# Output projection of an attention layer: weights streamed in by output block instead of loaded whole before it

## The chip, the cores and the metric

The kernel runs on the 8 cores of one Trainium2 chip. All cores run the same program, each on its own batch element, with no exchange between them. The metric is the device time in microseconds of the slowest core.

## The reference, cut to what matters

```python
x = x + 0.5 * ffn(layernorm(x))      # low-rank FFN, gelu
x = x + attn(layernorm(x))           # causal, 16 heads of 64
x = x + 0.5 * ffn(layernorm(x))

# the last step of attn, the one that the change touches:
attn = jnp.einsum('bhqk,bkhd->bqhd', scores, v)
return jnp.einsum('bqhd,hdm->bqm', attn, O_w) + O_b
```

The input is 8 x 2048 x 1024 in float32: one sequence of 2048 positions and 1024 features for each core. `O_w` is 1024 x 1024 when its heads are flattened, `O_b` has 1024 elements.

## The kernel before, in words

The residual stream `x` stays in SBUF for the whole program as [128 partitions, 8 feature chunks, 2048 positions] in float32. The program is a sequence of stages: FFN sublayer `f1`, the attention sublayer, FFN sublayer `f2`, and the output DMAs. Each stage is made of `nc.Block()` regions. In a block each engine (TensorE, VectorE, ScalarE, GpSimd and SyncE, which issues all DMAs) has its own instruction list, written out by hand; within a block the lists are tied together only by semaphores, and at the end of a block all engines meet in a barrier before any of them goes on.

The attention sublayer (`emit_attn_sublayer`, from L1076 on) ends in eight head pairs (`emit_attn_pair`, one block each, L604). The last thing that the last pair does is to normalise its last 512 positions and to write them into `attn_fm` (L768), a bf16 tensor [128, 8 chunks of head features, 2048 positions] that holds the attention result.

Then comes the output projection, in three blocks:

- `load_stage` (from L335 on) with four pieces of `ow`, 1 MB each (two chunks of 128 rows, all 1024 output columns, so that every descriptor's row of `ow` is read in full). The staging tile `wst3` has room for exactly one piece, so SyncE's load of a piece (L360) waits for the cast of the piece before it (the wait at L359). VectorE casts each piece to bf16 into `wb2` (L373), which holds the whole weight.
- `load_stage` once more for the bias `ob`, 4 KB, cast into `r_ob`.
- The projection block (from L1361 on). Its order is eight output blocks `m` of 128 features, and in each the four position tiles of 512. One tile is eight matmuls over the chunks of `attn_fm` (L1374) and one of the bias (L1376) into one half of a double buffer in PSUM. VectorE then adds the tile to `x` (L1387), which frees the half (semaphore `EV`); TensorE signals each finished tile through `PE`. Output block `m` needs the columns 128m to 128m+127 of `ow` alone.

In the trace's rows the buffer numbers are left out, so `wb2` reads as `wb` and `wst3` as `wst`. After the projection block comes the statistics block of `f2` (loads at L208, first casts at L251).

One further load of the same form as the changed ones is in the kernel before: in each head pair SyncE loads 128 columns of `kw` into `wst4` as [128, 8, 128] (L857) once the cast of the `qw` piece (L799) has freed the buffer, and VectorE casts it (L802) when it has landed.

Of the kernel before, what the change touches and what calls it, by code (L numbers as in the profile page):

```python
# [8 lines left out]
BF16 = mybir.dt.bfloat16  # L9
# [5 lines left out]
D = 1024  # L15
NT = S // 128
NC = D // 128
# [13 lines left out]
def build_nc(debug=()):  # L31
    nc = bass.Bass("TRN2", target_bir_lowering=False, dynamic_dma_scratch_size=2048)

    din = {}
# [22 lines left out]
    def mk(stack, name, shape, dt=F32, psum=False):  # L57
        uid[0] += 1
        f = nc.psum_tensor if psum else nc.sbuf_tensor
        if _dbg_alloc and not psum:  # L60
            nb = int(np.prod(shape[1:])) * (4 if dt == F32 else 2)
            _tot[0] += nb

            @contextlib.contextmanager
            def _wrap(nb=nb, nm=name):
                with f(f"{nm}_{uid[0]}", shape, dt) as t:
                    print(f"+ {nm:12s} {nb:7d} tot={_tot[0]}")
                    try:
                        yield t
                    finally:  # L70
                        _tot[0] -= nb
                        print(f"- {nm:12s} tot={_tot[0]}")
            return stack.enter_context(_wrap())
        return stack.enter_context(f(f"{name}_{uid[0]}", shape, dt))

    with gctx:
# [20 lines left out]
        class _H:  # L97
# [9 lines left out]
        LD, CAST, PE, EV, ACT, ROW, ST, DMX, WC, WP = (_H(sems[k]) for k in  # L107
            ["ld", "cast", "pe", "ev", "act", "row", "st", "dmx", "wc", "wp"])
        LSL = [_H(sems[f"l{i}"]) for i in range(10)]
# [225 lines left out]
        def load_stage(stage, pairs, scale=None):  # L335
            views = []
            half = stage.shape[-1] // 2
            for i, (src_ap, dst_ap) in enumerate(pairs):
                fs = list(src_ap.shape[1:])
                tot = int(np.prod(fs))  # L340
                npart = src_ap.shape[0]
                if tot <= half and len(pairs) > 1:
                    sv = stage[0:npart, half * (i % 2):half * (i % 2) + tot]
                else:
                    sv = stage[0:npart, 0:tot]
                if len(fs) == 2:
                    sv = sv.rearrange("p (a b) -> p a b", a=fs[0])
                views.append(sv)
            dbl = all(int(np.prod(p[0].shape[1:])) <= half for p in pairs) and len(pairs) > 1
            with nc.Block() as blk:  # L350
                ld0, cast0 = LD.v, CAST.v
                n = len(pairs)

                @blk.sync
                def _(sync):
                    if not dbl:
                        for i in range(n):
                            if i >= 1:
                                sync.wait_ge(CAST.h, cast0 + i)  # L359
                            LD.inc(sync.dma_start(views[i], pairs[i][0]), 16)  # L360
                    else:
                        for g in range((n + 1) // 2):
                            if g >= 1:
                                sync.wait_ge(CAST.h, cast0 + 2 * g)
                            for i in (2 * g, 2 * g + 1):
                                if i < n:
                                    LD.inc(sync.dma_start(views[i], pairs[i][0]), 16)

                @blk.vector
                def _(vector):  # L370
                    def cast_one(i):
                        if scale is None:
                            CAST.inc(vector.tensor_copy(pairs[i][1], views[i]))  # L373
                        else:
                            CAST.inc(vector.tensor_scalar(pairs[i][1], views[i], scale, None, OP.mult))
                    if not dbl:
                        for i in range(n):
                            vector.wait_ge(LD.h, ld0 + 16 * (i + 1))
                            cast_one(i)
                    else:  # L380
                        for g in range((n + 1) // 2):
                            hi = min(n, 2 * g + 2)
                            vector.wait_ge(LD.h, ld0 + 16 * hi)
                            for i in range(2 * g, hi):
                                cast_one(i)
# [690 lines left out]
        def emit_attn_sublayer():  # L1076
            with contextlib.ExitStack() as actx:
# [30 lines left out]
                with nc.Block() as blk:  # L1108
                    @blk.sync
                    def _(sync):  # L1110
                        LD.inc(sync.dma_start(ct["m2t"][:, :], din["masksb"].ap()[1]), 16)
                        sync.wait_ge(LD.h, LD.v)
# [55 lines left out]
                with contextlib.ExitStack() as vctx:  # L1168
# [21 lines left out]
                    with nc.Block() as blk:  # L1190
                        pe0, ev0, row_lc, ld_vb = PE.v, EV.v, ROW.v, LD.v
# [42 lines left out]
                        def _(vector):  # L1234
# [53 lines left out]
                            for _, fn in sorted(dvepl, key=lambda x: x[0]):  # L1288
                                fn(vector)
# [60 lines left out]

                bctx.close()
                with contextlib.ExitStack() as octx:
                    wb2 = mk(octx, "wb2", [128, NC, D], BF16)
                    r_ob = mk(octx, "r_ob", [1, D], BF16)
                    wst3 = mk(octx, "wst3", [128, 2048])
                    load_stage(wst3, [(din["ow"].ap().rearrange("(c p) m -> p c m", p=128)
                                       [:, 2 * i:2 * (i + 1), :], wb2[:, 2 * i:2 * (i + 1), :])
                                      for i in range(4)])
                    load_stage(wst3, [(din["ob"].ap(), r_ob[0:1, :])])

                    with nc.Block() as blk:  # L1361
                        pe0, ev0 = PE.v, EV.v

                        @blk.tensor
                        def _(tensor):
                            i = 0
                            for m in range(NC):
                                for tci in range(NTC):
                                    if i >= 2:
                                        tensor.wait_ge(EV.h, ev0 + i - 1)  # L1370
                                    sl = slice(TC * tci, TC * (tci + 1))
                                    psl = p_big[:, 512 * (i % 2):512 * (i % 2) + TC]
                                    for hc in range(NC):
                                        tensor.matmul(psl, wb2[:, hc, 128 * m:128 * (m + 1)],  # L1374
                                                      ct["attn_fm"][:, hc, sl], start=(hc == 0), stop=False)
                                    PE.inc(tensor.matmul(psl, r_ob[0:1, 128 * m:128 * (m + 1)],  # L1376
                                                         r_ones[0:1, 0:TC], start=False, stop=True))
                                    i += 1

                        @blk.vector  # L1380
                        def _(vector, pe0=pe0):
                            i = 0
                            for m in range(NC):
                                for tci in range(NTC):
                                    vector.wait_ge(PE.h, pe0 + i + 1)
                                    sl = slice(TC * tci, TC * (tci + 1))
                                    EV.inc(vector.tensor_tensor(x[:, m, sl], x[:, m, sl],  # L1387
                                                                p_big[:, 512 * (i % 2):512 * (i % 2) + TC],
                                                                OP.add))
                                    i += 1  # L1390
# [12 lines left out]
        if PHASES >= 2:  # L1403
            emit_attn_sublayer()
            if "x2" in dbg:
                emit_dump_fm(dbg["x2"], x)
# [47 lines left out]
```

## Time and profile before

| | us |
|---|---|
| median of 2 runs | 2037.53 |
| lowest, highest | 2034.7, 2040.36 |
| profiled execution, its own time | 2036.73 |
| span of its slowest core (core 5) | 2035.2 |
| span of its fastest core (core 0) | 1995.6 |

| busy on core 5 | us | share of the span |
|---|---|---|
| TensorE matmuls (PE) | 1568.7 | 77% |
| VectorE (DVE) | 571.2 | 28% |
| ScalarE (ACT) | 557.2 | 27% |
| GpSimd (POOL) | 95.3 | 5% |

A span runs from a core's first instruction to its last. The profiled execution's own time is 1.5 us above the span of its slowest core. PE is TensorE's matmuls and PEld its weight loads. PEclk is the granted clock of TensorE: 1.00 is 2.4 GHz and 0.50 is 1.2 GHz, and a mean in between is a mixture of the two.

### The profile page before, as it was taken

What the parts mean: (1) busy time and instruction counts of PE and PEld (TensorE: products, weight loads), DVE (VectorE), ACT (ScalarE), POOL (GpSimd) and SP (SyncE); (2) the same over time, 40 slices, a digit from 0 to 9 for tenths busy, and PEclk for the clock granted to TensorE, in tenths of its full rate; (3) what the DMA queues carried; (4) which work ended last, traced back from release to release, by engine and by line L of the source; (5) the groups of instructions that cost most, each with busy time, mean ns of one, the idle gap of its engine ahead of it and who ended that gap; (6) DMA issues with size and microseconds to landing.
All of it is one profiled execution on the core that took longest, in us unless ns stands there. A gap on an engine that the chain in (4) does not pass through costs nothing. (4 is left out here: it accounts for less than half of the span.)

```text
span 2035.2 us, 17874 instructions; the slowest of 8 cores (1995.6 to 2035.2 us)
## 1 busy us (share of the span) xinstructions
PE 1568.7 (77%) x5640; PEld 418.2 (21%) x5640; DVE 571.2 (28%) x952; ACT 557.2 (27%) x615; POOL 95.3 (5%) x108
## 2 busy tenths in 40 slices
PE   2389997567759698696997969969798396599994
PEld 0022222122212122121221212212111131122220
DVE  2522211752402414123142241322401236421111
ACT  1232222200023334333333333333344003222320
POOL 0100000001001001010010100101000002000000
PEclk7598998779858768587575876858655696788986
DMA  8300000300120200102001020010000206000004
GB/s 265 109 0 0 1 1 7 97 32 24 39 62 1 52 0 11 42 1 53 0 11 42 1 52 0 11 32 1 21 0 0 83 0 207 1 1 0 1 0 165
DMA packets 63752, 72.69 MB, mean 36 GB/s; under 512 B 20487, under 2 KB 51351, under 8 KB 61614
## 3 DMA queue, kind: packets, MB, share of 16 engines
q1 hardware_dynamic: 63662, 71.54, 12.0%
q8 instruction: 50, 0.82, 0.2%
q14 instruction: 40, 0.33, 0.1%
HBM read 50.49 MB, written 12.58 MB: 31 GB/s over the span
## 5 line engine op out<-in xcount | busy, mean ns | idle before, releaser
L725 ACT ACTIVATE pt<-p_big 128x1024 bf16<-128x1024 f32 (+3 forms) x320 | 286.5, 895 | 596.9 <-PE p_big L686 336.4
L680 PE MATMUL p_big<-qgA,kgA 65*128 65x512 bf16 (+3 forms) x320 | 150.8, 471 | 123.0 <-ACT pt L725 63.8
L570 ACT ACTIVATE hb<-p_big 128x1024 bf16<-128x1024 f32 x128 | 130.9, 1024 | 310.0 <-PE p_big L493 308.1
L491 PE MATMUL p_big<-pb,v1b 128*128 128x512 bf16 x512 | 158.8, 393 | 14.4 <-DVE pb L528 14.4
L639 PE MATMUL p_big<-pt,v_pair 128*64 128x512 bf16 (+3 forms) x320 | 158.9, 497 | 0.0
L642 PE MATMUL p_big<-pt,v_pair 128*64 128x512 bf16 (+3 forms) x320 | 158.2, 494 | 0.0
L686 PE MATMUL p_big<-qgB,kgB 65*128 65x512 bf16 (+3 forms) x320 | 157.4, 492 | 0.0
L635 PE MATMUL p_big<-pt,ones_bf 128*1 128x512 bf16 (+3 forms) x320 | 156.0, 487 | 0.0
L631 PE MATMUL p_big<-pt,ones_bf 128*1 128x512 bf16 (+3 forms) x320 | 146.9, 459 | 0.2
L501 PE MATMUL p_big<-hb,u2b 128*128 128x512 bf16 x512 | 136.0, 389 | 4.7 <-ACT hb L570 4.7
L230 PE MATMUL p_big<-xb_s,ones_bf 128*1 128x512 bf16 x96 | 51.5, 537 | 78.5 <-DVE xb_s L251 78.3
L493 PE MATMUL p_big<-r_ones,r_b 1*128 1x512 bf16 x256 | 100.9, 394 | 0.0
L534 DVE CAST qmb<-p_big 128x1024 bf16<-128x1024 f32 x8 | 9.8, 1225 | 278.2 <-PE p_big L501 278.2
L1374 PE MATMUL p_big<-attn_fm,wb 128*128 128x512 bf16 x256 | 63.0, 390 | 30.7 <-PEq L350 30.7
L680 PEld LDWEIGHTS p_big<-qgA,kgA 65*128 65x128 bf16 x320 | 32.2, 101 | 260.2 <-issue 260.2
L745 DVE CAST rdsb<-rdf 1x1024 bf16<-1x1024 f32 x32 | 21.7, 679 | 208.6 <-ACT rdf L712 208.6
L639 PEld LDWEIGHTS p_big<-pt,v_pair 128*64 128x64 bf16 x320 | 38.2, 119 | 192.8 <-issue 190.9
L942 PE MATMUL p_big<-yb,wqb 128*128 128x512 bf16 x256 | 72.0, 432 | 4.8 <-DVE qp L1014 4.8
L541 DVE TENSOR_TENSOR x<-x,p_big 128x1024 f32<-128x1024 f32 x32 | 39.1, 1221 | 115.6 <-PE p_big L515 115.6
L1228 PE MATMUL p_big<-wb,yb 128*128 128x512 bf16 x256 | 65.4, 402 | 3.0 <-DVE vaug_r L1252 1.5
L1029 DVE TENSOR_REDUCE u_sc<-p_big 1x1 f32<-1x512 f32 x96 | 65.3, 680 | 8.7 <-DVE u_sc L1033 0.8
L942 PE MATMUL p_big<-yb,wkb 128*128 128x512 bf16 x256 | 60.7, 380 | 6.6 <-DVE kp L1014 4.8
(149 smaller groups left out, 1570.0 us busy)
## 6 DMA issues: line engine op xcount, KB each, us to landing
wstage<-u SPq DMA_DIRECT2D x40, 256.0 KB, 5.7
wstage<-v SPq DMA_DIRECT2D x40, 256.0 KB, 5.4
x<-xT SPq DMA_DIRECT2D x8, 1024.0 KB, 10.8
outT<-x SPq DMA_DIRECT2D x8, 1024.0 KB, 10.7
wstage<-vw SPq DMA_DIRECT2D x16, 256.0 KB
vscr<-vb_s SPq DMA_DIRECT2D x32, 128.0 KB
v_pair<-vscr SPq DMA_DIRECT2D x8, 512.0 KB
wst<-ow SPq DMA_DIRECT2D x4, 1024.0 KB
```

The lines of the kernel that those rows point to most:

```text
L491: tensor.matmul(psl, v1b[:, rc, 128 * fc:128 * (fc + 1)], pb[:, c % 2, rc, :], start=(rc == 0), stop=False)
L493: PE.inc(tensor.matmul(psl, r_b1[0:1, 128 * fc:128 * (fc + 1)], r_ones[0:1, 0:TC], start=False, stop=True))
L501: PE.inc(tensor.matmul(p_big2[:, 512 * m:512 * m + TC], u2b[:, fc, 128 * m:128 * (m + 1)], hb[:, fc % 4, :], start=(fc == 0), stop=(fc == ...
L570: ACT.inc(scalar.activation(hb[:, 2 * (fp % 2):2 * (fp % 2) + 2, :], psl.rearrange("p (a b) -> p a b", a=2), AF.Gelu_apprx_tanh))
L631: tensor.matmul(p_big[base:base + 1, 1024 + lo - 512 * c:1024 + hi - 512 * c], ones_bf[:, 0:1], pt[:, 0, sl, 0:w], start=(kt == 0), stop=s ...
L635: tensor.matmul(p_big[base:base + 1, 1536 + lo - 512 * c:1536 + hi - 512 * c], ones_bf[:, 0:1], pt[:, 1, sl, 0:w], start=(kt == 0), stop=s ...
L639: tensor.matmul(p_big2[0:64, lo:hi], vp[:, kt, 0:64], pt[:, 0, sl, 0:w], start=(kt == 0), stop=stop, tile_position=(0, 0), skip_group_chec ...
L642: mm = tensor.matmul(p_big2[64:128, lo:hi], vp[:, kt, 64:128], pt[:, 1, sl, 0:w], start=(kt == 0), stop=stop, tile_position=(0, 64), skip_ ...
L680: mm = tensor.matmul(p_big[:, 0:w], kgA[:, ksl], qgA[:, lo:hi], start=True, stop=not first)
L686: mm = tensor.matmul(p_big[:, 512:512 + w], kgB[:, ksl], qgB[:, lo:hi], start=True, stop=not first)
L725: ch["XA"].inc(scalar.activation(pt[:, :, i % 2, 0:w], p_big[:, 0:1024].rearrange("p (a b) -> p a b", a=2)[:, :, 0:w], AF.Exp))
L942: tensor.matmul(psl, wb_[:, c, :], yb2[:, c, sl], start=(c == 0), stop=False)
```

## The change

The two `load_stage` calls are gone. The weight is cut by output block instead of by chunk of rows: eight pieces of 512 KB, each [128 partitions, 8 chunks, 128 columns]. Both the staging tile `wst3` and the bf16 tile `wb2m` hold two pieces, used in turn. Everything happens inside the projection block:

- SyncE issues piece 0 and the bias `ob` (into a tile of its own, `obst`) at the start of the block, and piece `m` once GpSimd has cast piece `m - 1`.
- GpSimd casts the bias, and then the eight pieces in order. The cast of piece `m` waits until piece `m` has landed and, from `m = 2` on, until TensorE has finished output block `m - 2`, whose half of `wb2m` it overwrites.
- TensorE waits for the bias cast once, and at the start of output block `m` for the cast of piece `m`. Its matmuls and their order are as before. VectorE no longer casts; its 32 additions are as before.

```diff
-                    wb2 = mk(octx, "wb2", [128, NC, D], BF16)
+                    wb2m = mk(octx, "wb2m", [128, 2, NC, 128], BF16)
+                    wst3 = mk(octx, "wst3", [128, 2, NC, 128])
                     r_ob = mk(octx, "r_ob", [1, D], BF16)
-                    wst3 = mk(octx, "wst3", [128, 2048])
-                    load_stage(wst3, [(din["ow"].ap().rearrange("(c p) m -> p c m", p=128)
-                                       [:, 2 * i:2 * (i + 1), :], wb2[:, 2 * i:2 * (i + 1), :])
-                                      for i in range(4)])
-                    load_stage(wst3, [(din["ob"].ap(), r_ob[0:1, :])])
+                    obst = mk(octx, "obst", [1, D])
+                    osrc = din["ow"].ap().rearrange("(c p) m -> p c m", p=128)
 
                     with nc.Block() as blk:
-                        pe0, ev0 = PE.v, EV.v
+                        pe0, ev0, row_o0 = PE.v, EV.v, ROW.v
+                        xl0 = [LSL[8].v, LSL[9].v]
+
+                        @blk.sync
+                        def _(sync):
+                            LSL[8].inc(sync.dma_start(
+                                wst3[:, 0, :, :], osrc[:, :, 0:128]), 16)
+                            LD.inc(sync.dma_start(obst[0:1, :], din["ob"].ap()), 16)
+                            for m in range(1, NC):
+                                sync.wait_ge(ROW.h, row_o0 + m + 1)
+                                LSL[8 + m % 2].inc(sync.dma_start(
+                                    wst3[:, m % 2, :, :],
+                                    osrc[:, :, 128 * m:128 * (m + 1)]), 16)
+
+                        @blk.gpsimd
+                        def _(gp):
+                            gp.wait_ge(LD.h, LD.v)
+                            ROW.inc(gp.tensor_copy(r_ob[0:1, :], obst[0:1, :]))
+                            for m in range(NC):
+                                gp.wait_ge(LSL[8 + m % 2].h,
+                                           xl0[m % 2] + 16 * (m // 2 + 1))
+                                if m >= 2:
+                                    gp.wait_ge(PE.h, pe0 + 4 * (m - 1))
+                                ROW.inc(gp.tensor_copy(wb2m[:, m % 2, :, :],
+                                                       wst3[:, m % 2, :, :]))
 
                         @blk.tensor
                         def _(tensor):
+                            tensor.wait_ge(ROW.h, row_o0 + 1)
                             i = 0
                             for m in range(NC):
+                                tensor.wait_ge(ROW.h, row_o0 + m + 2)
                                 for tci in range(NTC):
...
-                                        tensor.matmul(psl, wb2[:, hc, 128 * m:128 * (m + 1)],
+                                        tensor.matmul(psl, wb2m[:, m % 2, hc, :],
```

The first order piece is SyncE's list between the last head pair and `f2`, with the semaphores that its instructions wait for (`wst_71` and `wst_70` are the staging tiles of before and of now; `s_row` counts GpSimd's casts).

```order
 L840 DMA kgB<-u_row 1x16x128
 L604 UNCONDITIONAL_BRANCH
-L354 UNCONDITIONAL_BRANCH [waits barrier_Pool_Activation_PE_DVE_SP_release]
-L360 DMA wst_71<-ow 128x2x1024
-L360 DMA wst_71<-ow 128x2x1024 [waits s_cast] x3
-L350 UNCONDITIONAL_BRANCH
-L354 UNCONDITIONAL_BRANCH [waits barrier_Pool_Activation_PE_DVE_SP_release]
-L360 DMA wst_71<-ob 1x1024
-L350 UNCONDITIONAL_BRANCH
+L1363 UNCONDITIONAL_BRANCH [waits barrier_Pool_Activation_PE_DVE_SP_release]
+L1365 DMA wst_70<-ow 128x8x128
+L1367 DMA obst<-ob 1x1024
```

Four loads of two full chunks, and behind a barrier the bias, have become one load of 128 columns with the bias right behind it; seven more loads of 128 columns, each behind a wait for a cast, follow in the same list.

The second is GpSimd's list at the same place (`s_l8` and `s_l9` are the two slots' load counters, `s_ld` the bias's, `s_pe` TensorE's count of finished tiles).

```order
 L604 UNCONDITIONAL_BRANCH
+L1374 UNCONDITIONAL_BRANCH [waits barrier_Pool_Activation_PE_DVE_SP_gather]
+L1377 CAST r_ob<-obst 1x1024 [waits s_ld]
+L1383 CAST wb2m<-wst_70 128x1024 [waits s_l8]
+L1383 CAST wb2m<-wst_70 128x1024 [waits s_l9]
+L1383 CAST wb2m<-wst_70 128x1024 [waits s_l8,s_pe]
+L1383 CAST wb2m<-wst_70 128x1024 [waits s_l9,s_pe]
```

GpSimd had nothing here before; now it has nine casts, the first of them the bias, ahead of the one on which TensorE's first matmul depends.

## Rows read from the trace of the kernel before

**Rows 1.** Core 5, in order of time: start us, us, instruction, idle before and releaser.
```profile
1581.91 0.69 DVE L768 TENSOR_TENSOR attn_fm<-p_big,rdb 128x512 bf16<-128x512 f32 x1
1582.88 20.06 SPq L360 DMA_DIRECT2D wst<-ow  x4
1588.34 1.23 DVE L373 CAST wb<-wst 128x2048 bf16<-128x2048 f32 x1 [5.74 <-DMA wst<-ow]
...
1607.49 1.23 DVE L373 CAST wb<-wst 128x2048 bf16<-128x2048 f32 x1 [4.99 <-DMA wst<-ow]
1608.99 0.25 SPq L360 DMA_DIRECT2D wst<-ob  x1
1610.60 0.68 DVE L373 CAST r_ob<-wst 1x1024 bf16<-1x1024 f32 x1 [1.89 <-DMA wst<-ob]
1611.61 3.57 PE L1374 MATMUL p_big<-attn_fm,wb 128*128 128x512 bf16 x8 [30.67 <-PEq L350]
```

**Rows 2.** Busy time by stretch of core 5: PE, PEld, DVE, ACT, POOL, PEclk, DMA share, GB/s.
```profile
1582.00:1611.70 29.70, 0.10 (x1) 0.13 (x2) 6.19 (x6) 0.00 (x0) 0.00 (x0) 0.50 0.41 141
1611.70:1682.00 70.30, 70.30 (x286) 25.50 (x286) 21.35 (x31) 0.00 (x0) 0.00 (x0) 0.96 0.00 1
```

**Rows 3.** Core 5, a head pair's `kw` load, VectorE and the DMA queue.
```profile
680.23 0.69 DVE L802 CAST wkb<-wst 128x1024 bf16<-128x1024 f32 x1 [4.25 <-DMA wst<-kw]
...
676.05 0.37 SPq L857 DMA_DIRECT2D wst<-kw  x1
```

**Rows 4.** Waits of core 5: waited for, us in total, times, longest us.
```profile
DVE wkb L802 <- DMA wst<-kw: 26.0, 6, 5.0
```

**Rows 5.** Issues from 560 to 580 us on core 5: KB each, us to landing; their issue times.
```profile
kgB<-kp SPq DMA_DIRECT2D x1, 256.0 KB, 6.4
kgA<-u_row SPq DMA_DIRECT2D x1, 4.0 KB, 5.2
...
571.99 1.42 SPq L838 DMA_DIRECT2D kgB<-kp  x1
573.45 0.59 SPq L839 DMA_DIRECT2D kgA<-u_row  x1
```

**Rows 6.** POOL by line and shape: busy us, mean ns of one, idle before.
```profile
L186 POOL CAST u2b<-wstage 128x512 bf16<-128x512 f32 x8 | 5.0, 626 | 29.2 <-DMA wstage<-u 29.2
L186 POOL CAST r_b<-wstage 1x512 bf16<-1x512 f32 x4 | 3.1, 780 | 5.0 <-DMA wstage<-b 5.0
L1121 POOL MEMSET ones_sr<- 1x1024 bf16 x1 | 0.9, 941 | 0.0
L122 POOL MEMSET r_ones<- 1x512 bf16 x1 | 0.5, 515 | 0.0
```

**Rows 7.** Core 5, tiles at the start of the projection, in order of time.
```profile
1615.64 2.39 PE L1374 MATMUL p_big<-attn_fm,wb 128*128 128x512 bf16 x8
1618.28 1.90 PE L1374 MATMUL p_big<-attn_fm,wb 128*128 128x512 bf16 x8
1620.43 1.90 PE L1374 MATMUL p_big<-attn_fm,wb 128*128 128x512 bf16 x8
```

**Rows 8.** Busy time of core 5 by stretches of 10 us, columns as in rows 2.
```profile
1560.00:1570.00 10.00, 10.00 (x29) 1.89 (x28) 0.00 (x0) 3.99 (x5) 0.00 (x0) 0.50 0.00 0
1620.00:1630.00 10.00, 10.00 (x43) 3.75 (x43) 3.44 (x5) 0.00 (x0) 0.00 (x0) 1.00 0.01 2
1820.00:1830.00 10.00, 10.00 (x22) 1.81 (x20) 2.44 (x2) 1.02 (x1) 0.00 (x0) 0.50 0.00 0
```

**Rows 9.** Spans of cores, and the projection's matmuls of cores 5 and 7.
```profile
core 5: 2035.2 us, clock 0.745
core 7: 2025.1 us, clock 0.745
...
L1374 PE MATMUL p_big<-attn_fm,wb x256: 379/379/634, 1611.6 to 1682.2; 128*128 128x512 bf16 x128
...
L1374 PE MATMUL p_big<-attn_fm,wb x256: 379/379/631, 1619.1 to 1689.2; 128*128 128x512 bf16 x128
```

## Prediction

> **What bounds the kernel now.** I began with the page's slices of the span: TensorE is busy nearly everywhere, with one slice just before 1600 us in which no compute engine does much and the DMA engines do. The timeline of that place [rows 1] shows why. The last result of attention is written from 1581.91 to 1582.60 us. SyncE issues the first piece of `ow` at 1582.88, VectorE starts its cast at 1588.34, and so on four times in strict turn, load and cast, because the staging tile holds one piece. The last weight cast ends at 1608.72, the bias takes another round to 1611.28, and TensorE's first matmul of the projection is at 1611.61. So from 1582.60 to 1611.61, 29.0 us, TensorE has nothing to do. The busy time by stretch [rows 2] confirms that nothing else covers it: between 1582.0 and 1611.7 VectorE has 6.19 us of work, which is the casts and the end of the last pair, ScalarE and GpSimd have none, and the DMA engines are at 41%. In the projection itself TensorE is busy 70.30 of 70.30 us with the DMA engines idle. The stretch in front of it is therefore wholly on the path that sets the end, on every core alike, since all of them meet a barrier at each block and share nothing. What could be hidden is the load, under a projection that uses neither DMA nor GpSimd.
>
> **The change part by part.** *Removed:* the whole chain from the issue at 1582.88 to the matmul at 1611.61, which is 28.73 us [rows 1]. That includes two barriers between blocks; the one from the last pair stays.
>
> *Added in its place, first the load of piece 0.* It has the form of the pair's `kw` load, 512 KB as [128, 8, 128]. That load was issued at 676.05 and its cast began at 680.23, so 4.18 us [rows 3]. The six waits for it on the same core come to 26.0 us, 4.3 each, the longest 5.0 [rows 4]; a wait begins with the cast before it, about 0.1 us ahead of the issue. I take 4.2. Before, all cores load `ow` at much the same time, and a piece of twice the bytes took 5.46 us (1582.88 to 1588.34), so the upper bound is 5.7; the lower one is 4.0.
>
> *The bias load behind it.* It is issued some 0.4 us later, on the same queue. The nearest case is a 4 KB row behind a 256 KB copy: the copy, issued at 571.99 with 6.4 us to landing, arrives at 578.4, and the row, issued at 573.45 with 5.2 us, at 578.65 [rows 5]. A small transfer thus arrives about 0.3 us behind the large one ahead of it. Against that stands the lone `ob` load, which needed 1.61 us from issue to cast (1608.99 to 1610.60, [rows 1]); by it the bias would land 2 us before piece 0. I take the first, 0.3 us after piece 0, because the first is the one with a large transfer ahead of it.
>
> *The casts on GpSimd.* No row shows a cast of 1024 elements per partition there. Casts of 512 take 626 ns, those of 512 on a single partition 780 ns on average [rows 6]. Doubling gives upper values of 1.25 and 1.56 us. The memsets show that the length does not count in full: 515 ns for 512 and 941 for 1024, a factor of 1.83 [rows 6], which gives 1.15 us for 626 ns. I take 1.2 us for each cast, 1.1 to 1.6 as the bounds. In front of the first matmul stand two of them in a row, bias and piece 0, if the bias lands last; one, if it lands early.
>
> *Sum to the first matmul:* 4.2 + 0.3 + 1.2 + 1.2 + 0.2 for two semaphores passed on (the step from cast to matmul through a whole barrier took 0.33, [rows 1]) = 7.1 us after the issue, against 28.73. The gain is 21.6 us. Lower end: 5.7 + 0.3 + 1.6 + 1.6 + 0.3 = 9.5 us, a gain of 19.2. Upper end: 4.0 + 1.1 + 0.1 = 5.2 us, a gain of 23.5.
>
> *Pieces 1 to 7.* The smaller pieces move at a lower rate: 512 KB in 4.18 us against 1 MB in 5.46 [rows 1, 3], so eight loads in a row would take 33 us where four took 22. The Trainium skill, DMA: Bandwidth & Descriptors, in "Rules for kernel authors", says the same, asking for transfers of 1 MiB and more; by it alone the change would be for the worse. What counts, however, is each load against the time of an output block. A tile at the full clock takes 2.15 us (1618.28 to 1620.43, [rows 7]), a block of four 8.6 us. Piece `m` is issued when piece `m - 1` is cast; load, cast and hand-over come to 4.2 + 1.2 + 0.4 = 5.8 us a piece. So piece 1 is ready 5.8 us after the first matmul and needed after at least 8.6, and in fact later, because the first tiles are slow: 4.03 us for the first, 2.64 for the second (1611.61, 1615.64, 1618.28; [rows 1, 7]), which makes the first block 11.0 us. From piece 2 on, the cast also waits for TensorE to be done with block `m - 2`; that leaves it a whole block, 8.6 us, for 1.2 us of work. The waits at the block starts thus cost nothing, and they would cost something only once a load took over about 7 us. What is queued behind TensorE's wait is the rest of the projection; behind SyncE's waits nothing but later pieces (the loads of `f2` come after the next barrier, as before); behind GpSimd's, nothing until `f2`.
>
> *VectorE:* its additions, 0.69 us in each 2.15 us, are unchanged, and the five casts it loses were on the removed chain, so they are counted already. *Matmuls:* the same 288 in the same order.
>
> *Clock:* TensorE's granted clock was already 0.50 before the gap, in 1560 to 1570 with the engine busy throughout, and 1.00 in 1620 to 1630 [rows 8]. So the slow first tiles, some 2.4 us above the pace, are paid before and after alike: zero, with +0 to −2.4 us if a gap of 7 us lets it rise sooner than one of 29.
>
> *Against the measurement:* the profiled execution took 2036.73 us for a span of 2035.2. Minus 21.6 gives 2015.1; it stood 0.8 below the median of 2037.53, by which it would be 2015.9. I forecast 2015.5 us, 1.1% less. A measurement of this kernel tells about 2% (41 us) from no change, so this counts as within 2%.
>
> **The rivals.**
>
> *A. The gap closes to about 7 us and nothing else moves:* 2015.5, own range 2011 to 2021 from the bounds above and the 3 us by which the runs of before lie from their median.
>
> *B. The clock falls out otherwise in `f2`.* From the projection's last matmul to the end of the span core 5 took 2035.2 − 1682.2 = 353.0 us, core 7 335.9 [rows 9], for identical work; the difference is in stretches such as 1820 to 1830 on core 5, where TensorE is busy for 10 of 10 us at 0.50 [rows 8]. Everything after the projection now starts 21.6 us earlier, and these stretches may fall on other cores. If core 7, the last to leave the projection, got core 5's 353 us: 1689.2 + 353.0 + 1.5 − 21.6 = 2022. If core 5 got core 7's 335.9 us, the slowest would be core 7 itself: 2025.1 + 1.5 − 21.6 = 2005. For it speaks the spread of 40 us between cores; against it, that the two runs of before are 5.7 us apart although the stretches must fall anew in each.
>
> *C. The pauses cool TensorE.* The block starts now hold waits for weights, and if pieces came late the engine would pause seven times. The price, from rows: a tile at the low clock takes 4.03 us instead of 2.15, so a projection that stayed at 0.50 would cost 32 x 1.88 = 60 us more: 2015.5 + 60 = 2076. With one slow tile and the mixed one after it at each of seven starts it would be 7 x 2.4 = 17 us: 2032. The Trainium skill, TensorE: Matmul & The Clock Gate, in "Loop structure matters more than you think", names a wait for a DMA in front of each group of matmuls as the pattern that keeps the clock low. Against this rival: with pieces ready 2.8 us or more ahead there is no pause, and a start within the projection would look like any tile start of before, where the clock held 1.00.
>
> *D. Slower than before: the loads can't keep pace.* The place is SyncE's chain of load, cast, load. If a load of 128-column rows took L us with eight cores at it, the chain runs at L + 1.6 us a piece, and from 7 us on it sets the pace instead of the 8.6 us block. The gain of 21.6 us is eaten when 7 x (L + 1.6) exceeds 60.2 + 2.4 + 21.6, at L = 10.4 us. At 12 us the kernel would be at 2015.5 + 7 x 13.6 − 62.6 = 2048. For it speaks only that piece and row are smaller than before; against it the 4.3 us of the same form, 5.0 at the longest, and that 512 KB in 8.6 us is 61 GB/s where 141 were moved in the old stretch [rows 2].
>
> *E. No gain,* because the start waits for something else, such as a barrier that also waits for a load: 2037. The order lists show no such wait; the block opens with the same barrier that the old load block had.
>
> **How the numbers follow.** A 0.70, B 0.20 (half above, half below), C 0.04, D 0.02, E 0.04. The range that holds 8 in 10 takes A whole and most of B: 2007 to 2026, the upper end longer for a slower first load and a light form of C. More than 2% faster would need 41 us, more than the whole gap of 29, so only a lucky clock on top: 0.03. More than 2% slower means 2078 or more, which is C in full or D with L above 16 us: 0.02. Within 2%: 0.95.
>
> **What would show it right or wrong.** In the profile after: the first matmul of the projection 6 to 9 us after the first `ow` issue; the wait of GpSimd's bias cast about as long as piece 0's load, and the piece cast right behind it; no wait of TensorE for GpSimd's casts but the first; PEclk at 1.00 from some 10 us into the projection to its end; the projection still about 70 us. Matmuls waiting at the start of each fourth tile would show C or D. A first matmul in place with a time above 2026 would show B: then the length of `f2` by core tells it. The prediction is wrong if the gap closes by less than 19 us.

## The result, and the profile after

| | before | after |
|---|---|---|
| median of the runs | 2041.56 us (10) | 2016.95 us (11) |
| ratio to before, 95% interval | | 0.9885 (0.9845 to 0.9925) |
| same pair on another chip | 2034.96 us | 2014.36 us, 0.991 (0.9877 to 0.9942) |
| profiled execution, slowest span | 2036.73, 2035.2 | 2014.83, 2013.3 |

The forecast was 2015.5 us and a ratio of 2015.5 / 2037.53 = 0.989. The kernel before has its median 4 us above the 2037.53 of the two runs that the forecast started from. Single runs of either kernel spread by more than a per cent, so the intervals hold gains between 12 and 32 us. What the change did is therefore read from the profile.

The place of the change on the slowest core of the profile after, in order of time, as in [rows 1]:

```profile
1585.86 0.69 DVE L768 TENSOR_TENSOR attn_fm<-p_big,rdb 128x512 bf16<-128x512 f32 x1
1586.83 0.39 SPq L1365 DMA_DIRECT2D wst<-ow  x1
1587.27 0.52 SPq L1367 DMA_DIRECT2D obst<-ob  x1
1590.84 1.03 POOL L1377 CAST r_ob<-obst 1x1024 bf16<-1x1024 f32 x1 [138.38 <-DMA obst<-ob]
1591.82 1.03 POOL L1383 CAST wb2m<-wst 128x1024 bf16<-128x1024 f32 x1
...
1593.00 3.57 PE L1398 MATMUL p_big<-attn_fm,wb2m 128*128 128x512 bf16 x8 [8.11 <-POOL wb2m L1383]
```

The last attention write ends at 1586.55 and the first projection matmul starts at 1593.00: a gap of 6.45 us where there were 29.0. The whole chain is in these rows: issue at 1586.83, bias there at 1590.84, two casts of 1.03 us end to end, matmul. The gap can be formed on every core of both profiles. Before it was 27.7 to 30.0 us, on average 28.7; after, 6.4 to 7.4 us, on average 6.8. That is 21.9 us less, and it agrees with the medians (24.6 and 20.6 us). The slowest spans of the two profiles also lie 21.9 us apart (core 5 before, core 3 after), but that they match so closely is chance: the gap gives 22.6 us, the projection 0.6 and the stage behind it 2.7, and the stages ahead of the projection, which the change does not touch, took 4.0 us more on core 3.

Who waited for whom from 1580 to 1665 us on that core (us in total, times, longest):

```profile
POOL wb2m L1383 <- PE p_big L1400: 43.3, 6, 7.6
...
PE p_big L1398 <- POOL wb2m L1383: 8.1, 1, 8.1
POOL wb2m L1383 <- DMA wst<-ow: 4.2, 1, 4.2
```

TensorE waited for a weight cast once, at the start. From piece 2 on it is GpSimd's cast that waits for TensorE, six times and 7.2 us each, with the next piece in staging. Busy time by stretch, with the columns of [rows 2]:

```profile
1593.00:1603.00 10.00, 10.00 (x35) 3.40 (x35) 2.06 (x3) 0.00 (x0) 1.04 (x1) 0.81 0.37 107
1603.00:1663.00 60.00, 60.00 (x253) 22.15 (x252) 19.21 (x28) 0.00 (x0) 6.24 (x6) 1.00 0.16 44
```

The loads now run under the projection at 44 GB/s, TensorE is busy without a break, and its granted clock is 1.00. The projection takes 69.3 to 70.4 us on the eight cores, against 69.2 to 70.7 before.

### The profile page after: what moved, and what is told of

Same layout as the page of the kernel before. It is cut to its first block and busy times, and to the rows that moved or that the text cites. A ratio compares the mean times of both kernels' runs of the same rounds, so it can differ in the third digit from the quotient of the medians.

```text
span 2013.3 us, 17883 instructions; the slowest of 8 cores (1968.4 to 2013.3 us)
## 1 busy us (share of the span) xinstructions
PE 1575.4 (78%) x5640; PEld 417.5 (21%) x5640; DVE 565.2 (28%) x947; ACT 556.8 (28%) x615; POOL 106.0 (5%) x117
## 3 DMA queue, kind: packets, MB, share of 16 engines
q1 hardware_dynamic: 70894, 71.54, 12.4%
## 5 line engine op out<-in xcount | busy, mean ns | idle before, releaser
L570 ACT ACTIVATE hb<-p_big 128x1024 bf16<-128x1024 f32 x128 | 130.9, 1024 | 318.3 <-PE p_big L493 314.0
L1398 PE MATMUL p_big<-attn_fm,wb2m 128*128 128x512 bf16 x256 | 62.5, 388 | 8.1 <-POOL wb2m L1383 8.1
L651 PE MATMUL p_big<-rdsb,r_ones 1*64 1x512 bf16 x64 | 16.9, 512 | 64.7 <-DMA kgB<-u_row 57.5
```

Of the source, the lines that this page charges most:

```text
L570: ACT.inc(scalar.activation(hb[:, 2 * (fp % 2):2 * (fp % 2) + 2, :], psl.rearrange("p (a b) -> p a b", a=2), AF.Gelu_apprx_tanh))
```

## The experiments

For each kernel the gap (end of the last attention write to the first projection matmul) and the projection (first to last weight matmul) are means over its eight cores, worked out like those above. A ratio compares with the kernel before on the same chip; its median there was 2041.56 us for the row "changed", 2036.1 for "bias cast second", "one bf16 slot", "three further loads ahead" and "whole weight first", and 2034.96 for the others. Times of different chips are therefore compared by their ratios only.

| kernel | gap | projection | time, ratio to before |
|---|---|---|---|
| before | 28.7 | 70.1 | |
| changed | 6.8 | 69.9 | 2016.95, 0.9885 (0.9845 to 0.9925) |
| changed, again | 6.6 | 69.9 | 2014.36, 0.991 (0.9877 to 0.9942) |
| bias cast second | 5.8 | 70.1 | 2010.13, one run |
| one bf16 slot | 6.6 | 80.4 | 2019.74, 0.9887 (0.9838 to 0.9935) |
| one further load ahead | 8.5 | 69.9 | 2015.27, one run |
| three further loads ahead | 12.4 | 86.9 | 2034.39, 0.9971 (0.9934 to 1.0009) |
| whole weight first, all at once | 15.3 | 70.3 | 2020.58, 0.991 (0.9878 to 0.9941) |
| pieces 0 and 1 in the last pair | see below | see below | 2008.01, 0.9859 (0.9834 to 0.9884) |
| and two tiles in the last pair | see below | see below | 2000.54, 0.9823 (0.9794 to 0.9852) |

**What the start consists of.** GpSimd casts piece 0 first and the bias behind it:

```diff
-                            gp.wait_ge(LD.h, LD.v)
-                            ROW.inc(gp.tensor_copy(r_ob[0:1, :], obst[0:1, :]))
                             for m in range(NC):
...
                                 ROW.inc(gp.tensor_copy(wb2m[:, m % 2, :, :],
                                                        wst3[:, m % 2, :, :]))
+                                if m == 0:
+                                    gp.wait_ge(LD.h, LD.v)
+                                    ROW.inc(gp.tensor_copy(r_ob[0:1, :], obst[0:1, :]))
...
-                            tensor.wait_ge(ROW.h, row_o0 + 1)
                             i = 0
                             for m in range(NC):
-                                tensor.wait_ge(ROW.h, row_o0 + m + 2)
+                                tensor.wait_ge(ROW.h, row_o0 + (m + 2 if m else 1))
...
+                                    if i == 0:
+                                        tensor.wait_ge(ROW.h, row_o0 + 2)
```

In SyncE's list the wait ahead of piece 1 is changed as well, so that it is still for the cast of piece 0.

> Edit: GpSimd casts piece 0 of the weight first and the bias behind it; TensorE waits for the bias only ahead of the first tile's bias matmul. Theory (the start is a chain of load, bias cast of 1.03 us, piece cast of 1.03 us, with the bias landing no later than piece 0): from the end of the last attention write to the first projection matmul 5.4 us instead of 6.45 on core 3 of the changed kernel, and 1.0 us less in the time, which a single time cannot show. Rival (piece 0 lands about as late as the end of the bias cast, which is hidden anyway): 6.4 us as now.

The gap fell from 6.8 to 5.8 us, 5.5 to 6.3 by core. On core 3:

```profile
1583.18 0.69 DVE L768 TENSOR_TENSOR attn_fm<-p_big,rdb 128x512 bf16<-128x512 f32 x1
1584.15 0.39 SPq L1365 DMA_DIRECT2D wst<-ow  x1
...
1588.28 1.04 POOL L1381 CAST wb2m<-wst 128x1024 bf16<-128x1024 f32 x1 [143.43 <-DMA wst<-ow]
1589.26 1.03 POOL L1385 CAST r_ob<-obst 1x1024 bf16<-1x1024 f32 x1
...
1589.46 3.15 PE L1398 MATMUL p_big<-attn_fm,wb2m 128*128 128x512 bf16 x7 [7.25 <-POOL wb2m L1381]
```

From 1583.87 to 1589.46 the gap is 5.6 us, 5.4 expected. Piece 0 is there 4.13 us after its issue, and the bias, issued 0.45 us later, was there no later than the end of the 1 us cast. So the bias cast stood on the path in the changed kernel, as the prediction's sum had it. The rival of this run, a late piece 0 that leaves the gap as it was, is out.

**Whether short pauses cool TensorE.** One bf16 slot instead of two:

```diff
-                    wb2m = mk(octx, "wb2m", [128, 2, NC, 128], BF16)
+                    wb2m = mk(octx, "wb2m", [128, NC, 128], BF16)
...
-                                if m >= 2:
-                                    gp.wait_ge(PE.h, pe0 + 4 * (m - 1))
+                                if m >= 1:
+                                    gp.wait_ge(PE.h, pe0 + 4 * m)
```

> Edit: the bf16 weight tile holds one piece instead of two, so the cast of piece m waits for output block m - 1. Theory (short pauses cost only their length): TensorE idles 1.03 us of cast and 0.2 us of hand-over at each of 7 block starts, 8.7 us in all, at a granted clock of 1.00 from 10 us into the projection on; projection 70 to 79 us, time 0.4% above the changed kernel, about 2026. Rival C of the prediction (pauses cool TensorE): the granted clock falls to 0.50 after pauses, first tiles of a block at 4.0 instead of 2.15 us, projection 87 us or more, time above 2034.

The slowest core, waits and then two stretches of the projection:

```profile
PE p_big L1398 <- POOL wb2m L1383: 18.1, 8, 8.0
```

```profile
1640.90:1645.90 5.00, 3.57 (x16) 1.26 (x15) 1.02 (x2) 0.00 (x0) 1.04 (x1) 1.00 0.32 88
1645.90:1650.90 5.00, 5.00 (x23) 1.91 (x22) 1.73 (x3) 0.00 (x0) 0.00 (x0) 1.00 0.06 17
```

Of 18.1 us of waits 8.0 are the start; the other seven are 10.1 us, 1.44 each, where 1.24 were expected. The busy time of 3.57 in 5.00 us shows one of them. The granted clock stays at 1.00 through all seven, and so it does on the other seven cores. So rival C finds nothing to stand on with these pauses: they make up 10.1 of the 10.5 us by which the projection is longer (80.4 against 69.9 us; 70 to 79 had been expected). The run also shows what the second slot buys, 10 us. The time of the kernel, with four runs, doesn't show these 10 us: its interval holds the changed kernel's ratio, and the median of 2019.74 us is 6 below the 2026 expected.

**When the stream stops being free.** Three, and in another kernel one, further loads of 512 KB ahead of each piece, into a tile that nobody reads:

```diff
+                            def more(m):
+                                for k in range(3):
+                                    DMX.inc(sync.dma_start(
+                                        extra[:, k, :, :],
+                                        osrc[:, :, 128 * ((m + k + 1) % NC):
+                                             128 * ((m + k + 1) % NC) + 128]), 16)
+                            more(0)
                             LSL[8].inc(sync.dma_start(
...
                                 sync.wait_ge(ROW.h, row_o0 + m + 1)
+                                sync.wait_ge(DMX.h, DMX.v)
+                                more(m)
...
```

> Edit: ahead of each piece SyncE issues three further loads of 512 KB of the same form into a tile that nobody reads, so a piece lands later. Theory (rival D of the prediction as a mechanism: the chain load plus 1.3 us sets the pace once a load takes over about 7 us): a piece lands 10 to 12 us after the first issue of its group, TensorE pauses 2.7 to 4.7 us at the block starts, projection 7 x 12.3 + 9 = 95 us (87 to 102), first matmul 7 us later, so 7 + 25 = 32 us above the changed kernel: about 2049, no faster than before. With the clock as a second effect (pauses of 3 to 4 us bring 0.50 back): blocks of up to 16 us, projection up to 125 us, about 2079. Rival (loads hide whatever they take): projection 70 us, only the start 7 us later, 2024.

> Edit: as the kernel with three further loads ahead of each piece, with one. Three of them made a piece's wait 10.0 us and the cycle 11.05 us, against 4.15 and 5.3 without. Theory (what counts is whether the cycle of load, cast and issue is above 8.6 us, the time of an output block): a wait of 5.5 to 6.5 us, a cycle of 7 to 7.7, no pause of TensorE at any block start but the first, projection 69 to 71 us, gap 8 to 9 us. Rival (every load that is slower than now shows up): pauses at the block starts.

With three, on the slowest core:

```profile
1609.47 1.04 POOL L1394 CAST wb2m<-wst 128x1024 bf16<-128x1024 f32 x1 [9.80 <-DMA wst<-ow]
...
1620.51 1.04 POOL L1394 CAST wb2m<-wst 128x1024 bf16<-128x1024 f32 x1 [10.00 <-DMA wst<-ow]
...
1621.80 3.46 PE L1409 MATMUL p_big<-attn_fm,wb2m 128*128 128x512 bf16 x8 [2.39 <-POOL wb2m L1394]
...
1631.58 1.04 POOL L1394 CAST wb2m<-wst 128x1024 bf16<-128x1024 f32 x1 [10.03 <-DMA wst<-ow]
```

A piece now lands 10.0 us after the cast before it, and the casts follow one another at 11.05 us (1609.47, 1620.51, 1631.58). That is above the 8.6 us of a block, and TensorE waits 2.4 us. The projection grows to 84.7 to 88.7 us and the start to 12.4; together that is 22.6 us more than in the changed kernel, which is the whole gain, and the ratio of 0.9971 (0.9934 to 1.0009) agrees. The prediction's rival D put that point at a load of 10.4 us, but its sum leaves out that a slow load delays piece 0 as well; with L − 4.2 us for the start it gives about 9.7 us. Of the 22.6 us measured, 17.0 are in the projection and 5.6 at the start. My expectation of 32 us was too high by 9, mostly because I took a cycle of 12.3 us, with 2.0 to 2.6 us for each of the three loads in front of a piece; they cost 1.95 ((10.0 − 4.15) / 3). The clock:

```profile
1614.80:1619.80 5.00, 4.61 (x19) 1.60 (x19) 1.65 (x3) 0.00 (x0) 0.00 (x0) 1.00 1.06 268
1619.80:1624.80 5.00, 3.00 (x8) 1.02 (x8) 0.41 (x1) 0.00 (x0) 1.04 (x1) 0.68 0.34 93
...
1639.80:1644.80 5.00, 2.68 (x13) 1.04 (x12) 1.05 (x2) 0.00 (x0) 1.04 (x1) 1.00 0.40 98
```

Here it falls behind two of the pauses (0.68 at 1619.8 and 0.66 at 1654.8), and not behind others that are as long. It is so on every core, with two or three falls each, and the length of the pause alone does not decide: on core 0 the first tile behind a pause of 2.99 us has its eight weight matmuls in 1.89 us, and one behind a pause of 2.75 us takes 3.15. So the effect that rival C names does occur in this kernel, now and then. TensorE does not set the pace here, so the slower tiles cost little: the cycle stayed at about 11 us across the fall (11.07 us, then 10.96). In the last block, which no cast follows, a slow tile does lengthen the projection.

With one further load, waits of the slowest core:

```profile
POOL wb2m L1394 <- DMA wst<-ow: 26.1, 4, 7.2
POOL wb2m L1394 <- PE p_big L1411: 22.2, 3, 7.6
...
PE p_big L1409 <- POOL wb2m L1394: 9.7, 1, 9.7
```

Where the cast waited for its piece, the wait was 6.5 us on average and at the most 7.2, half as long again as before, and TensorE waits for none but the first; the projection is 69.9 us on average, that of the changed kernel. So up to about 7 us a slower load costs nothing here but at the start, and at 10 us it costs the whole gain. That the border is the length of a block less cast and hand-over fits both; no run lies between them.

**How much the load had to do with order, and how much with its place.** The kernel before, with its whole weight still loaded ahead of the projection, but all four loads and the bias issued at once (VectorE's casts, in the same new block, are not shown):

```diff
-                    wst3 = mk(octx, "wst3", [128, 2048])
-                    load_stage(wst3, [...])
-                    load_stage(wst3, [(din["ob"].ap(), r_ob[0:1, :])])
+                    wst3 = mk(octx, "wst3", [128, NC, D])
...
+                            for s in range(4):
+                                LSL[s].inc(sync.dma_start(wst3[:, 2 * s:2 * s + 2, :],
+                                                          osrc[:, 2 * s:2 * s + 2, :]), 16)
+                            LD.inc(sync.dma_start(obst[0:1, :], din["ob"].ap()), 16)
...
```

> Edit to the kernel before: the whole weight is still loaded and cast ahead of the projection, but all four loads and the bias are issued at once into a staging tile of 32 KB per partition, and VectorE casts each as it lands. Theory (two parts: the strict turn of load and cast, and the 4 MB themselves, which no staging hides ahead of the projection): the last 1 MB lands 12 to 15 us after the first issue, cast 1.2, bias cast 0.7, barrier 0.3: a gap of 15 to 18 us from the last attention write to the first projection matmul, against 29.0 before and 6.45 changed; time 12 us below before, about 2029. Rival (the turn of load and cast is all there was to gain): a gap of 8 us or less and about 2018.

```profile
1587.35 2.20 SPq L1364 DMA_DIRECT2D wst<-ow  x4
...
1592.57 1.23 DVE L1372 CAST wb<-wst 128x2048 bf16<-128x2048 f32 x1 [5.50 <-DMA wst<-ow]
...
1600.24 1.23 DVE L1372 CAST wb<-wst 128x2048 bf16<-128x2048 f32 x1 [1.31 <-DMA wst<-ow]
1601.38 0.67 DVE L1375 CAST r_ob<-obst 1x1024 bf16<-1x1024 f32 x1
1602.37 1.87 PE L1390 MATMUL p_big<-attn_fm,wb 128*128 128x512 bf16 x4 [16.97 <-PEq L1358]
```

The casts follow each other at 2.56 us now, where a turn of load and cast took 6.4 in [rows 1] ((1607.49 − 1588.34) / 3). The gap is 15.3 us on average. So of the 21.9 us that the change took away, 13.4 were the strict turns, and 8.5 came from moving the load under the projection. About 2 of the 13.4 are the bias's own turn behind a barrier: its cast ended 2.56 us after the last weight cast in [rows 1] and 0.58 us after it here. The gap is as expected, the time (2020.58) 8 us lower than expected, 5.5 of which is the lower median of the kernel before on this chip. Its interval and those of the changed kernel overlap, and they don't rank the two.

**Beyond the changed kernel.** First, pieces 0 and 1 and the bias are loaded and cast in the last head pair. The bf16 pieces and piece 0's staging go into tiles that are idle there; the staging tiles of piece 1 and of the bias are new:

```diff
+                    if last:
+                        LD.inc(sync.dma_start(ct["obst"][0:1, :], din["ob"].ap()), 16)
+                        for m in range(2):
+                            LSL[8 + m].inc(sync.dma_start(
+                                ct["ws"][m], osrc[:, :, 128 * m:128 * (m + 1)]), 16)
...
+                ct["wm"] = [ct["wqb"], ct["wkb"]]
...
```

> Edit to the changed kernel: pieces 0 and 1 and the bias are loaded and cast in the last head pair, into tiles that are free there (the q/k weight tiles and their staging); the projection block starts with piece 2's load. Theory (the remaining 6.4 to 7.4 us of gap are load, two casts and hand-over, all of it movable): gap from the last attention write to the first projection matmul 0.6 to 1.0 us, the barrier alone; projection 70 us; 6 us or 0.3% below the changed kernel, ratio to the kernel before about 0.9865. Rival (the loads or casts disturb the last pair, or the shorter gap changes the clock): gap closed as said, but attention's last pair longer or the projection's first tiles faster or slower by some us.

```profile
1580.10 0.69 DVE L772 TENSOR_TENSOR attn_fm<-p_big,rdb 128x512 bf16<-128x512 f32 x1
...
1581.26 3.07 PE L1411 MATMUL p_big<-attn_fm,wqb 128*128 128x512 bf16 x7 [2.13 <-PEq L604]
```

From 1580.79 to 1581.26 there is 0.47 us, the barrier; it is 0.5 us on six cores and 0.8 us on the other two. The last pair's end is no longer than before: from its last attention matmul's start to the end of the last attention write it takes 7.6 us on average in both. From that write's end to the start of the last addition to `x` it is 71.3 us on average over the eight cores, against 77.3 in the changed kernel on the same chip. These 6.0 us are what the theory had, and the medians are 6.4 us apart.

Second, two tiles of the projection are also computed inside the last pair, around the last normalisation's matmuls (`ptile` holds the eight weight matmuls and the bias matmul of a tile):

```diff
+                        tensor.wait_ge(ROW.h, ct["row_o0"] + 3)
+                        tensor.wait_ge(ch["DR"].h, dr0 + off_dr + 2)
+                        ptile(0)
                         emit_bc(tensor, bc0 + off_bc + 9, False)
+                        ptile(1)
...
```

> Edit to the previous kernel of this call: the first two tiles of the projection (positions 0 to 1023, already normalised) are computed inside the last head pair, one ahead of the broadcast matmuls of the last normalisation, in TensorE's wait of 4.6 us for VectorE, and one behind them; their results wait in PSUM and are added to x in the projection block. Theory (TensorE waits 7.6 us in the end of the last pair for ScalarE and VectorE, and a tile at the low clock takes 4.0 us): the last attention write comes 0 to 1 us later, the projection block is 2 tiles or 6.7 us shorter (4.0 and 2.6 us at the clock's start) if the clock starts as before, in all 5 to 7 us less than the previous kernel of this call; ratio to the kernel before about 0.984. Rival (the clock's rise comes at the same number of tiles either way and the tile ahead of the broadcasts delays them): 2 us or less.

The slowest core, the last pair's end and the block's start:

```profile
1574.94 0.40 PE L651 MATMUL p_big<-rdsb,r_ones 1*64 1x512 bf16 x2 [2.48 <-DVE rdsb L765]
...
1575.49 1.90 PE L704 MATMUL p_big<-attn_fm,wqb 128*128 128x512 bf16 x8
...
1576.53 0.69 DVE L785 TENSOR_TENSOR attn_fm<-p_big,rdb 128x512 bf16<-128x512 f32 x1
...
1578.18 1.89 PE L1427 MATMUL p_big<-attn_fm,wqb 128*128 128x512 bf16 x8 [0.47 <-PEq L604]
```

The last attention write is no later for the tiles but 0.4 us earlier, 7.2 us after the last attention matmul's start instead of 7.6: with a tile of work in front, the broadcast matmuls (L651) take 0.40 us for two instead of 0.64. From that write's end to the start of the last addition to `x` it is 66.0 us on average over the cores, 5.3 less than with the loads alone moved. Together that is 5.7 us, of the 5 to 7 expected; the medians are 7.5 us apart. On core 5 of the two kernels (loads alone, then with the tiles) the last addition starts here, after a write that ended at 1580.79 and at 1581.37:

```profile
1651.62 0.69 DVE L1424 TENSOR_TENSOR x<-x,p_big 128x512 f32<-128x512 f32 x1 [1.46 <-PE p_big L1413]
```

```profile
1646.99 0.69 DVE L1441 TENSOR_TENSOR x<-x,p_big 128x512 f32<-128x512 f32 x1 [1.46 <-PE p_big L1429]
```

The kernel with the tiles beats both the changed one and the one with the loads alone moved, by 34.4 us or 1.8% against the one before. It computes the reference in full, as does the one above.

## Why the prediction was right

- **The place and the size.** The stretch from 1582.60 to 1611.61 was on the path of every core, and what is left of it is 6.8 us. Forecast gain 21.6 us, measured 21.9 in the gaps. The agreement to 0.3 us is in part luck: the new chain came out 0.6 us shorter than its sum on average, and the old gap of core 5, from which I reckoned, was 0.4 us above the average.
- **Load of piece 0.** Taken as 4.2 us from a load of the same form elsewhere. In the changed kernel its landing is hidden behind the bias cast; with the cast order swapped it was there 4.0 to 4.9 us after its issue, 4.3 on average and 4.1 on core 3. Rows of the same form, found in another stage, were the right source, and not the 5.46 us of a piece of another form in the same place.
- **Bias load.** Taken as 0.3 us behind piece 0 by [rows 5]. The bias cast began 3.9 to 5.0 us after piece 0's issue, 4.2 on average, so on average no later than piece 0 came in the swapped kernel: nothing to add. The lone `ob` load of [rows 1] was no guide either, by which it would have come 2 us before. The sign that the prediction named for it, the length of GpSimd's wait, can't be used: the row says 138.4 us, since GpSimd had been idle long before the issue.
- **Casts.** Taken as 1.2 us each, measured 1.03. With these small misses the chain from issue to matmul is 6.17 us (1586.83 to 1593.00) instead of 7.1, so the sum was 0.9 us too cautious on that core. Two of them in a row was right, and the run with the cast order swapped shows it. VectorE casts the same shape in 0.69 us [rows 3] and has nothing else to do at the start; whether casting there would shorten it no run shows.
- **Waits at the block starts.** Forecast free up to a load of about 7 us: at 6.5 us on average they are free, at 10 us they and the later start cost the whole gain. Rival D's 10.4 us lay close to that although its sum left the start out.
- **Clock of the projection.** Forecast unchanged: 69.9 us against 70.1. Rival C didn't occur, since there were no pauses; with seven pauses of 1.44 us there was no fall, with pauses of 2.1 to 3.3 us there was, now and then. The Trainium skill, TensorE: Matmul & The Clock Gate, in "Loop structure matters more than you think", warns of a long wait for a DMA in front of the matmuls, in which the engine stands idle. The changed source has a wait of that kind, for a cast behind a DMA, in front of each output block; in the trace it is over before TensorE reaches it, except at the start, and from 5 us into the projection on the granted clock is 1.00 on every core.
- **Rival B, the clock in `f2`.** The shifts did happen, but they nearly cancelled in the slowest core: 353.0 us behind the projection before (core 5), 350.3 after (core 3). The spans after the projection, for the same code, by the rows of the projection's matmuls in the profile after:

```profile
core 0: 1995.2 us, clock 0.769
...
core 5: 1996.2 us, clock 0.751
...
L1398 PE MATMUL p_big<-attn_fm,wb2m x250: 379/379/634, 1574.1 to 1643.4; 128*128 128x512 bf16 x125
...
L1398 PE MATMUL p_big<-attn_fm,wb2m x256: 379/379/634, 1591.6 to 1661.1; 128*128 128x512 bf16 x128
```

Core 5, which needed 353.0 us from there to its end before, needed 335.1 (1996.2 − 1661.1) now; core 0 went from 334.8 to 351.8. Over the cores the range is 334.8 to 353.3 us before and 335.1 to 351.8 after. The mean granted clock of that stretch went from 0.79 to 0.84 on core 5 and from 0.84 to 0.81 on core 0, so the slow stretches fell on other cores. What decides where they fall, no run shows. Something similar is seen ahead of the projection, where the code is unchanged: the last attention write ends between 1560.4 and 1589.3 us by core before, and between 1554.6 and 1586.6 after. Such shifts are at least part of why single runs spread, and why a change of 1% needs the profile.

## What to carry to other kernels

A weight that is loaded whole ahead of a stage, behind barriers and through a one-piece staging tile, costs its full chain of loads and casts with every compute engine idle. Cut it by what the consumer needs first, and stream the rest one piece ahead; smaller and slower transfers don't matter as long as load, cast and hand-over fit into the time that the consumer spends on one piece. Then look at what is left of the start: moving the first pieces into the stage before, and first tiles into its last wait, gave another 14 us here by the medians, and 11.7 in the profiled places.

## What I had not expected

A load of 512 KB queued behind three others of its kind took only 1.95 us more for each one ahead (2.35 us behind a single one), where alone it takes 4.1. So about half of a single load's time overlaps with the loads around it, and in the same way four loads of 1 MB issued at once arrived 2.56 us apart and not 5. GpSimd's cast of 1024 elements per partition takes 1.03 us on one partition and on 128 alike, and twice the length of the 512-element cast (626 ns, [rows 6]) would have been 1.25. And three kernels whose gap or projection differs by 8 to 10 us, one of them on another chip (two slots, one slot, whole weight at once) gave ratios of 0.991, 0.9887 and 0.991: by time alone none could have been told from the others.
